# Gathering every tile of a graph propagation from GpSimd's queue, with six PSUM banks and one-hots six tiles ahead

## The reference

```python
h = acc = emb                                        # N x 128
for _ in range(2):
    h = segment_sum(adj_val[:, None] * h[adj_col], adj_row, num_segments=N)
    acc = acc + h
graph_item_embs = acc / 3
combined = graph_item_embs[items] + item_features[items]
seq_hidden = take_along_axis(combined, alias_inputs[..., None], axis=1)
...                                                  # tanh, sigmoid, weighted sum -> sess_emb
scores = (12 * l2norm(sess_emb)) @ l2norm(graph_item_embs).T
```

## Time and profile before

| | us |
|---|---|
| three timed runs | 6086.2, 6096.6, 6096.9 (median 6096.6) |
| span of the profiled execution | 6020.2 |
| layer 1, first to last sum (780.8 to 3235.9) | 2455.1 |
| layer 2, first to last sum (3274.6 to 5568.8) | 2294.2 |
| busy in the span: PE, DVE, POOL, ACT | 3070.2, 3014.4, 2890.1, 866.4 |

### The profile page before, as it was taken

One profiled execution on the slowest core, in us unless ns is written; L12 is line 12 of the kernel. 1 busy time (PEld: TensorE's weight loads), 2 busy tenths in 40 slices (PEclk: granted clock), 3 DMA queues, 4 the chain that ended last, 5 costly groups with the idle time before them and its releaser, 6 DMA issues.

```text
span 6020.2 us, 68764 instructions
## 1 busy us (share of the span) xinstructions
PE 3070.2 (51%) x9778; PEld 1849.5 (31%) x9778; DVE 3014.4 (50%) x7257; ACT 866.4 (14%) x3005; POOL 2890.1 (48%) x2965
## 2 busy tenths in 40 slices
PE   5988744444444444444444444444444444445578
PEld 3777622222222222222222222222222222222344
DVE  8999754444444444444444444444444444445455
ACT  2998800000000000000000000000000000000543
POOL 1666654444444444444445454454454454455561
PEclk8888866666666666666666666666666666666689
DMA  0000011111111111111114111111111111112454
GB/s 25 4 3 3 3 48 33 32 31 32 32 31 33 33 34 33 34 33 31 32 32 120 34 37 35 33 37 36 32 37 35 33 37 35 34 36 80 79 84 139
DMA packets 162229, 235.35 MB, mean 39 GB/s; under 512 B 67554, under 2 KB 107776, under 8 KB 161952
## 3 DMA queue, kind: packets, MB, share of 16 engines
q0 software_dynamic: 92896, 171.14, 12.4%
q1 hardware_dynamic: 54132, 58.90, 3.0%
q10 hardware_dynamic: 15052, 3.83, 0.3%
HBM read 192.69 MB, written 41.01 MB: 39 GB/s over the span
## 4 chain that ended last, share of the span: by engine, by line
ACTq 49%; issue 32%; DVE 7%; PE 6%; ACT 3%; another core or an unknown queue 2%; POOL 1%; DMA 0%; DVEq 0%; SPq 0%; POOLq 0%
ACTq L686 43%; ACTq L682 5%; ACT big L644 2%; PE bank L1520 1%; PE bank L1382 1%; POOL sorted_edges L542 1%; DVE stage L944 1%; PE bank L1548 1%; DVE acc L1167 1%; DVE big L888 1%; PE bank L1507 1%; DVE ring L896 0%; PE bank L1482 0%; DVE big L904 0%
## 5 line engine op out<-in xcount | busy, mean ns | idle before, releaser
L1444 PE MATMUL bank<-ring 128*128 128x256 f32 x4976 | 2105.7, 558 | 2135.8 <-DVE ring L1118 1194.1
L1444 PEld LDWEIGHTS bank<-ring 128*128 128x128 f32 x4976 | 1147.7, 263 | 3071.0 <-DVE ring L1118 1662.5
L574 POOL DMA_INDIRECT ring<-in_L_rec_emb,cring x1195 | 1134.9, 950 | 1336.2 <-ACT cring L662 978.9
L1167 DVE TENSOR_TENSOR acc<-acc,bank 128x256 f32 x2488 | 1029.6, 414 | 1481.3 <-remote 1131.6
L1118 DVE TENSOR_SCALAR ring<-bank,mlo,mval 128x256 f32<-128x256 f32 x2488 | 1343.5, 540 | 742.4 <-DMA ring<-in_L_rec_emb 523.1
L574 POOL DMA_INDIRECT ring<-table,cring x1195 | 1130.2, 946 | 1202.8 <-PE bank L1444 795.7
L644 ACT ACTIVATE big<-big 128x68 f32<-128x68 bf16 x1764 | 557.7, 405 | 1.2 <-issue 1.2
L1382 PE MATMUL bank<-big,ring 128*128 128x136 f32 x2352 | 430.8, 328 | 75.5 <-issue 20.8
L542 POOL DMA_INDIRECT sorted_edges<-moved,block_to x313 | 397.2, 1269 | 100.3 <-issue 100.0
L1382 PEld LDWEIGHTS bank<-big,ring 128*128 128x128 f32 x2352 | 356.8, 219 | 147.6 <-ACT big L644 83.2
L660 ACT COPY mlo<-ring 128x24 f32 (+1 forms) x104 | 21.7, 209 | 2415.0 <-issue 2381.6
(11 more groups left out here) (213 smaller groups left out, 1700.7 us busy)
## 6 DMA issues: line engine op xcount, KB each, us to landing
ring<-in_L_rec_emb SPq DMA_DIRECT2D x3136, 0.5 KB
ring<-in_L_rec_emb ACTq DMA_DIRECT2D x3136, 0.5 KB
ring<-table ACTq DMA_DIRECT2D x3136, 0.5 KB
ring<-table SPq DMA_DIRECT2D x3136, 0.5 KB
scores<-stage SPq DMA_DIRECT2D x48, 512.0 KB
ring<-in_L_rec_emb,cring POOLq DMA_INDIRECT x1195
ring<-table,cring POOLq DMA_INDIRECT x1195
table<-big SPq DMA_DIRECT2D x7, 896.0 KB, 9.1
```

Of the source, the lines that this page charges most:

```text
L574: pool.indirect_dma_start(msg[:, s, :], None, source, bass.IndirectOffsetOnAxis(cring[:, s:s + 1], 0)).then_inc(s_g[s], 16)
L1167: add = dve.tensor_tensor(acc[:, bass.ds(off, BUCKET)], acc[:, bass.ds(off, BUCKET)], bank[u % PR][:, 0:BUCKET], ALU.add)
L1444: pe.matmul(bank[u % PR][:, 0:BUCKET], msg[:, h * T + u, :], onehot[:, u % SR, :], start=True, stop=True).then_inc(s_mm[u % M], 1)
```

## The change

`is_own`, the row-by-row fetches on SP and ACT, their semaphores, the lists of addresses and the three DVE instructions that make them are taken out. POOL gathers all 1244 tiles of a layer, and every one-hot waits on its slot's gather semaphore. The products rotate through six PSUM banks instead of four, the one-hots are built six tiles ahead instead of four (the ring of eight one-hots stays), and the two transposed embedding blocks share bank 6.

```diff
-    SR, PR, LEAD = 8, 4, 4
+    SR, PR, LEAD = 8, 6, 6
     PACE, AHEAD = 8, 12
...
-    FED = [sum(1 for j in range(u, NU, 2 * T) if not is_own(j)) for u in range(2 * T)]
+    FED = [len(range(u, NU, 2 * T)) for u in range(2 * T)]
...
@@ SP
-            sp.wait_ge(s_mrdy, 3)
-            own_tiles(0, emb_bytes)
...
-            own_tiles(1, table1_bytes)
...
@@ POOL, gather_step
                     s = h * T + u
-                    if is_own(T * c + u):
-                        continue
                     if u % PACE == 0:
...
@@ ACT
-            act.wait_ge(s_mrdy, 3)
-            own_rows(emb_bytes, 0, 1)
             with act.Fori(1, NST // 2 - 1) as i:
                 for h in range(2):
                     fetch(0, 2 * i + h, h)
-                    own_rows(emb_bytes, i * (2 * HALF) + HALF * (h - 1), h)
...
                     emb_rows(2 * i + h, h)
                     fetch(1, 2 * i + h + 2, h)
-                    own_rows(table1_bytes, i * (2 * HALF) + HALF * (h + 1), h)
...
@@ DVE
-            dve.wait_ge(s_lines, 32)
-            link(dve.tensor_copy(own_at.rearrange("o (k s) -> o k s", k=NOWN), own_lines[:, :, :, 0]))
-            link(dve.tensor_single_scalar(own_at, own_at, BUCKET.bit_length() - 1, ALU.arith_shift_right))
-            dve.tensor_single_scalar(own_at, own_at, LINE.bit_length() - 1, ALU.logical_shift_left).then_inc(s_mrdy, 1)
...
-                if u % T < T - 1:
-                    dve.wait_ge(s_g[u], 16 * (FED[u] * layer + it + 1))
-                elif isinstance(it, int) and not is_own(2 * T * it + u):
-                    dve.wait_ge(s_g[u], 16 * (FED[u] * layer + (FED[u] if it else 1)))
-                else:
-                    dve.wait_ge(s_line[u // T], 16 * P)
-                    dve.sem_clear(s_line[u // T])
+                dve.wait_ge(s_g[u], 16 * (FED[u] * layer + it + 1))
...
-                                  bank[5 + h][:, 0:2 * D], ALU.add).then_inc(s_ea, 1)
+                                  bank[6][:, 2 * D * h:2 * D * (h + 1)], ALU.add).then_inc(s_ea, 1)
@@ PE
-                    last = pe.transpose(bank[5 + h][:, q * D:(q + 1) * D], gnr[:, h, q, :], ident[:, :])
+                    last = pe.transpose(bank[6][:, (2 * h + q) * D:(2 * h + q + 1) * D], gnr[:, h, q, :], ident[:, :])
```

More of the change, by code:

```diff
@@ L23 @@
 I16 = mybir.dt.int16
-U8 = mybir.dt.uint8
 P = 128
@@ L78, in recommender_program @@
     FAR = float(2 ** 20)
-    SR, PR, LEAD = 8, 4, 4
+    SR, PR, LEAD = 8, 6, 6
     PACE, AHEAD = 8, 12
-    LINE = 4 * D
-    HALF, AT_ONCE = P // 2, 32
-    NOWN = NST - 3
     M = 4
@@ L92, in recommender_program @@
     OPEN, NORMS = 5, 8
-    assert NST // 2 - 1 == L // 2 and HALF % AT_ONCE == 0 and NST % 2 == 0
-    assert NT <= N and NST % 2 == 0 and SG % Q == 0 and D == P and 0 < TAIL < P and T % SR == 0 and SR % PR == 0 and LEAD <= PR
+    assert NST // 2 - 1 == L // 2 and NST % 2 == 0
+    assert NT <= N and NST % 2 == 0 and SG % Q == 0 and D == P and 0 < TAIL < P and T % SR == 0 and T % PR == 0 and LEAD <= PR and LEAD + 2 <= SR
     LOOP = 2 * min(NST // 2 - 1, L // 2, NB // 2)
@@ L103, in recommender_program @@
     TC = [T * (NST * n // 3) for n in range(4)]
-    HELD = "a column is held between 0 and N - 1, and an unused slot's is its tile's number, below NT <= N; a line has 512 bytes"
     FITS = "a tile's offset is 256 times the buckets that begin at or before it, less one: 0 to ROWS - 256"
-    def is_own(j):
-        return j % T == T - 1 and 1 <= j // T <= NOWN
-    FED = [sum(1 for j in range(u, NU, 2 * T) if not is_own(j)) for u in range(2 * T)]
+    FED = [len(range(u, NU, 2 * T)) for u in range(2 * T)]
     assert T % 4 == 0 and max(TC[n + 1] - TC[n] for n in range(3)) <= 512
@@ L168, in recommender_program @@
         sorted_rows = big[:, 0:-(-NT // P) * 2 * P].rearrange("p (m s w) -> p m s w", w=2, s=P)
-        at[0] = -(-NT // P) * 2 * P
-        own_lines = carve(big, NOWN * HALF * 2)[0:2, :].rearrange("o (k s w) -> o k s w", k=NOWN, w=2)
-        assert at[0] <= ROWS
         at[0] = 0
@@ L230, in recommender_program @@
         block_at_l = carve(stage, NKL * P)
-        own_at = stage[0:2, 6 * D:6 * D + NOWN * HALF].bitcast(I32)
-        assert 6 * D + NOWN * HALF <= 4 * 512 * 2
         assert at[0] <= 4 * 512 * 2
@@ L340, in recommender_program @@
         s_iota = sem("s_iota")
-        s_lines = sem("s_lines")
-        s_line = [sem(f"s_line{h}") for h in range(2)]
         s_g = [sem(f"s_g{u}") for u in range(2 * T)]
@@ L397, in recommender_program @@
         s_out = [sem(f"s_out{i}") for i in range(4)]
-        emb_bytes = emb.rearrange("n d -> (n d)").bitcast(U8)
-        table1_bytes = table1.rearrange("n d -> (n d)").bitcast(U8)
-        msg_bytes = [msg[:, (h + 1) * T - 1, :].bitcast(U8) for h in range(2)]
         block = ctx.enter_context(nc.Block())
@@ L703, in _ @@
                 fetch(1, c, c)
-            act.wait_ge(s_t1w, 16 * (NB // GRP))
-            own_rows(table1_bytes, 0, 1)
             act.wait_ge(s_eld, 32)
```

## The result

The changed kernel takes 4848.9 us (median of 4 runs, 4844.7 to 4851.4) against 6092.8 us of the kernel before in the same session (4 runs, 6086.2 to 6096.9). The ratio is 0.7959, with a 95% interval of 0.7947 to 0.7970. I forecast 4900 us, in a range of 4440 to 5200. The profiled execution took 4851.1 us, with a span of 4849.3.

The account below looks back on a forecast made before the run. ACT's row fetches were taken as the bound, then DVE and PE's loop at 1.43 us a tile: layers 4749.3 to 3555 us, plus 5 ahead, saves 1199; 6096.6 - 1199 = 4898, say 4900 us, range 4440 to 5200.

Parts of the forecast that it names:

- ACT's sequencer bounds the kernel before: In the layers, ACT's 64 row DMAs a chunk take 45.6 us and set the pace, 1.98 and 1.85 us a tile.
- About 14 us after gathers begin to stream, the rest slows down: In a burst of 23 gathers, register moves and sums slow after about 14 us, recovering some 4 us after the last.
- 0.78 + 0.60 + 0.04: DVE and PE's loop, us a tile: undisturbed sums, DVE's waiting ahead of them, chunk-end work; 1.42, taken as 1.43.
- C: Theory from the experiments, not rival C: something outside POOL serves one gather in some 1.42 us, starving others when POOL issues faster.
- Rival A: In the layers, POOL is the bound at 1.25 us a tile, PE's slow completions gone or hidden: 4450 us; chance 22%.
- Rival B: In the layers, congestion becomes permanent without pauses on ACT's fetch: 1.92 us a tile gives 6115 us, 2.1 gives 6563; chance 3%.
- rival C: In the layers, congestion partly permanent: 1.55 to 1.90 us a tile, 5200 to 6060 us; chance 11%.
- Six banks, six tiles ahead: PE's product banks and DVE's one-hot lead: counted as nothing, since more queued matmuls move the queue and not its rate.
- ACT's copies and the shared bank 6: ACT's three 0.2 us copies a chunk no longer come late; embedding blocks sharing a bank cost nothing, at most 20 us.
- Ahead of the layers: Before the first one-hot, dropping three DVE address instructions saves 5.3 us, counted as 5.
- The carry-over of 76.4 us: Timed median above profiled span in the kernel before, added unchanged to the predicted span of 4821 us.

## Why the prediction was right, step by step

- **ACT's sequencer bounds the kernel before: right.** It left the chain with its rows; half the rows gave most of the gain.
- **"About 14 us after gathers begin to stream, the rest slows down": misread.** The rest slows far sooner. ACT's register moves, 29 ns long up to 1958.6, take some 700 from 1959.6 on, 7 us behind the first gather of the earlier trace rows; least, median and most of that stretch:

```profile
L686 ACTq MOVE ring<-in_L_rec_emb x5: 29/696/708, 1958.6 to 1965.2; - x5
```

  Over the 48 chunks of layer 1 with a burst of 23 gathers, the first slow move on ACT or SP comes 4.5 to 6.9 us behind the first gather in nine of ten. The sums go on for a while longer, which is what I had read. The forecast did not hang on the 14 us.
- **"0.78 + 0.60 + 0.04": the right sum, with a term that isn't what I took it for.** I read 0.60 as a stall that each gather brings and that adds to the loop. The idle time did come out (1493.0 against about 1500), and the step too (1.437 and 1.431 against 1.43). But with the lead of 9 tiles the 0.60 is 0.35 (878.3 / 2488) and with POOL at 1.60 us it is 0.07 (168.1 / 2488). So the stall is no cost of a gather but, by C, the difference between the rate at which gathers are served and the loop's own pace. What made the forecast good was that I took the level from 44 tiles without row fetches, 1.445, which by C were already held to that rate; I did not know it then, and that is luck.
- **Rival A's floor of 1.25 us.** POOL's own pace was never reachable: a gather that POOL could issue every 1.14 us (16 rows) was served no faster. The floor to look for was 1.42. The earlier trace rows nearly give it, but they are one burst. From the first gather to the last slow move on ACT or SP, divided by 23, the 48 bursts of layer 1 give 1.29 to 1.41, median 1.38, and this one is among the highest (1.41). In layer 2, where POOL itself waits within a burst, it is 1.32 to 1.54. The reading gives a floor that may be 3 to 10% low, not the figure.
- **Rival B's permanent congestion, and rival C between: neither came.** The steps of 1.437 and 1.431 are below both. POOL waited 62 to 66 times a layer, and sums came 0.78 us apart again behind such a wait, as in the earlier trace rows; that a POOL that waits stops feeding the congestion, and so keeps the mean near the rate, is my reading, not tested by itself.
- **"Six banks, six tiles ahead: I count nothing": wrong, and luck hid it.** With this many gathers they are worth 128 us (2.6%). I reasoned that congested matmuls come out one at a time, so that only the rate counts. With four banks POOL's waits rose from 237 and 234 us to 321 and 260 a layer (what its starts stand apart beyond 1.25 us, where that is over 0.5), and the step to 1.505 and 1.459. Why POOL waits more there was not tested; that tiles come free later is the likely reason. All rows that I sized the step from are those of a kernel with four banks. By them I said 1.43, and with four banks it would have been 1.48 on the mean; six banks, which I put at nothing, took the difference back. Two errors of about 0.05 us a tile, some 120 us, cancelled.
- **ACT's copies and the shared bank 6: nothing.** DVE's 18.1 us ahead of the one-hots leave room for no more there. Sharing bank 6 was not tried by itself; in the kernel before it came with a gain of 0.2%.
- **Ahead of the layers: 5 us saved.** From first gather to first sum it was 24.4 us before (756.4 to 780.8) and is 17.9 (768.3 to 786.2). The sort ahead of it ended 12 us later than in the profile before, so the first sum came 5.4 us later all the same.
- **The carry-over of 76.4 us: wrong.** The timed median after is no longer than the span (4848.9 and 4849.3). The span came out 28 us above my 4821: 10 in the layers (3564.7 against 3555), 11 before, 4 between and 4 behind them. The two errors, 76 too many and 28 too few, with 3 us of rounding are the 51 between 4900 and 4849. The profiled execution of the kernel before is faster than all its timed runs, and the kernel before with six banks, whose profiled execution is one of its timed runs (span 6098.3), shows where: its first gather comes 14 us later than in the earlier trace rows's trace (770.5 against 756.4) and its layers take 61 us longer (4809.6 against 4748.3, start to start). Most of the 76.4 us thus lay in the stretches that the sum replaced, and should not have been carried over; 12 of the 14 ahead of the layers did carry over. This is an argument from a kernel with other banks. Why that one execution was faster is not known.

What stays open: what serves the gathers at 1.42 us. The time was shown to depend on the number of gathers and not on their bytes or rows, and hardly on TensorE's instructions (1.2% for twice as many). The pace from which the stalls go lies between POOL's 1.28 us (congested) and 1.60 us (not); that it is the 1.42 is an inference from the steps. C also does not say why moves slow already 6 us into a burst, when by 1.25 against 1.42 us the gathers are less than 1 us behind (an estimate: five gathers of 0.17 us each). The sixteen increments of each gather and what POOL writes for each queue are candidates; no run here tells them apart.

## What to carry to other kernels

Before a queue is given more work, divide the length of a busy stretch, up to where the others have recovered, by the number of transfers in it. Do it for many stretches; here one gave 1.41 and the median of 48 was 1.38, for a floor near 1.42. If that is longer than the issuer's own spacing, suspect that this is the floor and the others' stalls its shadow: here they could be moved to another wait, and went only with fewer gathers or a slower POOL. Then fewer transfers help (half of them took the layers from 1.43 to 0.86 us a tile), smaller ones don't, and extra buffers can still be worth something, here 2.6%. To know whether a stall is a price or a shadow, slow the issuer down and look whether it goes.

## What the runs showed of the hardware

- A gather from GpSimd had a price in the whole core's time, 1.43 us, that its own duration (943 ns, or 838 with 16 rows) and its bytes (177.57 or 34.90 MB on the queue) don't show.
- Issued faster than that (1.25 or 1.28 us apart, and not at 1.60), gathers slowed what they have nothing to do with: the hand-over of matmuls, up to 5.6 us from sum to sum, and in the kernel before the register moves between ACT's row DMAs, from 29 to 700 ns. The changed kernel has no such moves; DVE's register instructions there stayed at 46 to 53 ns. Durations of DVE's and POOL's own instructions stayed nearly as they were: a sum took 414 ns in the changed kernel and 412 with the slower POOL, where hardly anything was late, and a gather 943 and 964.
- The granted clock of TensorE does not explain the late sums: in the layers it was 0.69 and 0.71 of 2.4 GHz in the changed kernel; with the slower POOL 0.52 and 0.51, near the lower of its two levels, 1.2 GHz, and the sums were on time. Where half the gathers had gone and TensorE was kept busy, it was 0.92 and 0.93.

The first layer with the slower POOL, and with every second tile gathered:

```profile
784.90:2796.30 2011.40, 1440.63 (x2476) 617.35 (x2476) 1111.45 (x2881) 21.78 (x150) 1679.64 (x3701) 0.52 0.16 40
...
785.20:1857.40 1072.20, 885.60 (x2476) 426.29 (x2476) 1014.61 (x2882) 21.81 (x150) 576.49 (x611) 0.92 0.15 38
```
